# Queries, keys and gates of passes 1 to 3 as products of rounded halves, a later GpSimd modulation, and another order at the end of the attention passes

## What is computed

```python
mod = (silu(c) @ wmod).reshape(4, 6, 1, 256)            # sa, ca, ga, sb, cb, gb
h = layernorm(x) * (1 + ca) + sa
q, k, v = h @ wq + bq, h @ wk + bk, h @ wv + bv          # 16 heads of 16
scores = einsum('bhnd,bhmd->bhnm', q, k) * dmask         # gamma_h ** (n - m), n >= m
ret = einsum('bhnm,bhmv->bhnv', scores, v)
norm = (ret - mean) * rsqrt(var + eps) * gn_w + gn_b     # per head, over tokens and features
x = x + ga * ((silu(h @ wg + bg) * norm) @ wo + bo)
h = layernorm(x) * (1 + cb) + sb
top, index = top_k(h @ gate_kernel, 2)                   # softmax over the two
x = x + gb * sum_e combine_e * (silu(h @ w0_e) * (h @ w1_e)) @ wo_e
```

## Time and profile before

| what | us |
|---|---|
| median of three runs | 408.42 (404.41 to 411.78) |
| the profiled execution | 404.26 |
| its span, first to last instruction | 402.4 |
| TensorE busy | 361.0 |
| VectorE busy | 259.8 |
| GpSimd busy | 231.3 |
| ScalarE busy | 173.4 |

### The profile page before, as it was taken

The page is one execution under the profiler, slowest core; times in us unless marked ns, Lnnn a source line. Parts: engine busy times, 40 slices in busy tenths (PEclk is TensorE's granted clock), DMA queues, the critical chain, the costliest instruction groups (busy, mean ns, idle before and its releaser), DMA issues.

```text
span 402.4 us, 11502 instructions
## 1 busy us (share of the span) xinstructions
PE 361.0 (90%) x3893; PEld 269.8 (67%) x3894; DVE 259.8 (65%) x728; ACT 173.4 (43%) x264; POOL 231.3 (57%) x173
## 2 busy tenths in 40 slices
PE   3897899899899878898995999999999999999980
PEld 3474556766766656556562778888888888888860
DVE  6458528756955884947662577777777777777740
ACT  3424336444463313352122265555555555555510
POOL 3112610754781746186574377777777877777751
PEclk9999999999999998999997999999999999999995
DMA  6955090165447433254696343333344343333222
GB/s 218 307 182 187 11 332 5 54 211 210 154 165 243 164 102 104 66 212 118 140 347 140 66 75 75 62 71 76 79 79 79 79 79 79 71 69 72 40 27 25
DMA packets 32322, 49.05 MB, mean 122 GB/s; under 512 B 3198, under 2 KB 18972, under 8 KB 32284
## 3 DMA queue, kind: packets, MB, share of 16 engines
q1 hardware_dynamic: 11384, 16.98, 15.7%
q0 software_dynamic: 8176, 13.65, 15.2%
q10 hardware_dynamic: 12724, 17.89, 13.2%
HBM read 30.35 MB, written 18.16 MB: 121 GB/s over the span
## 4 chain that ended last, share of the span: by engine, by line
PE 44%; DMA 4%; DVE 2%; issue 2%; POOL 2%; ACT 1%; POOLq 1%; ACTq 0%; SPq 0%; DVEq 0%
PE ps L1719 15%; PE ps L1700 7%; PE ps L1699 7%; PE ps L1703 7%; PE ps L1711 4%; PE ps L1690 3%; DMA out_dram<-wg_s,qd 2%; PE ps L1606 2%; DMA routed<-z 1%; POOL routed L567 1%; DMA out_dram<-wg_s,wv_s 1%; DMA rowbuf<-routed 1%; ACT h_last L712 1%; DVE vd L1111 0%; POOLq L130 0%
## 5 line engine op out<-in xcount | busy, mean ns | idle before, releaser
L599 POOL TENSOR_TENSOR w_lo<-we,w_hi 128x1024 fp32r<-128x1024 f32 x31 | 77.0, 2484 | 25.2 <-ACT w_hi L825 23.0
L1719 PE MATMUL ps<-we,qeo 128*128 x312 | 76.5, 388 | 2.2 <-DVE wg_s L1317 1.3
L1719 PEld LDWEIGHTS ps<-we,qeo 128*128 128x128 f32 x312 | 57.3, 191 | 20.3 <-issue 13.4
L809 ACT COPY qeo<-ps 128x512 f32<-128x512 f32 x39 | 22.9, 587 | 111.0 <-PE ps L1711 111.0
L609 POOL DMA_INDIRECT out_dram<-wg_s,qd x30 | 46.9, 1563 | 34.3 <-issue 14.6
L1324 DVE TENSOR_TENSOR w_halves<-we,w_halves 128x1024 fp32r<-128x1024 f32 x31 | 38.0, 1225 | 8.3 <-ACT w_halves L825 8.3
L1296 DVE CAST rT_halves<-ps 128x256 fp32r<-128x256 f32 x31 | 13.2, 424 | 39.7 <-PE ps L1606 39.7
L567 POOL DMA_INDIRECT routed<-h_first,idx x24 | 24.9, 1038 | 15.3 <-DVE idx L1158 8.6
L825 ACT CAST w_hi<-we 128x1024 fp32r x31 | 32.6, 1052 | 0.0
L825 ACT CAST w_halves<-we 128x1024 fp32r x31 | 32.5, 1048 | 0.1
L1690 PE MATMUL ps<-we,xn 128*128 x64 | 31.9, 623 | 0.3 <-issue 0.3
(11 more groups left out here) (237 smaller groups left out, 709.0 us busy)
## 6 DMA issues: line engine op xcount, KB each, us to landing
rowbuf<-routed SPq DMA_DIRECT2D x37, 260.5 KB, 3.0
we<-in_ffn_w_kernel_dram ACTq DMA_DIRECT2D x16, 512.0 KB, 4.3
we<-in_ffn_wo_kernel_dram ACTq DMA_DIRECT2D x8, 512.0 KB, 6.7
routed<-z ACTq DMA_DIRECT2D x9, 260.5 KB, 4.0
xs<-in_attn_x_dram SPq DMA_DIRECT2D x4, 512.0 KB, 11.3
out_dram<-xs ACTq DMA_DIRECT2D x4, 512.0 KB, 3.6
we<-in_wmod_dram SPq DMA_DIRECT2D x1, 1024.0 KB, 10.4
sbcb<-gsc_dram SPq DMA_DIRECT2D x4, 256.0 KB, 4.8
```

What stands on the lines that cost most here:

```text
L599: g.tensor_tensor(w_lo[1], expert_up(e, 1), w_hi[1].bitcast(F32), ALU.subtract)\
L1719: last = mm(down_ps, eit[s % 2][:, k, :], weights(e, 2 * FT * F + k * D, D), start=k == 0, stop=k == KF - 1)
```

## The change

Queries, keys and gates of passes 1 to 3 (all but the last gate projection of pass 3) are computed from rounded halves. In pass 0 ScalarE copies the three weights to a rounded form (`projection_halves`) and GpSimd makes their remainders (`weight_remainders`). In each later pass ScalarE makes rounded features `hT_hi` ahead of `hT`, and VectorE the remainder `hT_lo` (`features_lo`), behind the second masks. `project_halves` is six matmuls. The halves lie in the places of experts 6 and 7, which are loaded only after the first gate of pass 3; TensorE's wait for the experts moves accordingly. GpSimd waits for `hT_lo` ahead of `modulate` in passes 1 and 2, and in pass 0 ahead of `scale_wo`.

The order also changes: `values(p, 0)` goes ahead of the first query; in pass 3 `second_normed` goes ahead of the first row loads, `table_rows(0)` behind the second masks, `values(3, 1)` ahead of `turn_h2`, and `turn_rows(0, 0)` behind `average`; `group_center` goes ahead of `take_rows(0, 0)`, `weighted(1, 1)` ahead of `choose_weights`, and the padding copies come four and four, after steps 4 and 5.

```diff
...
         w_hi, w_lo = [w0_halves[:, 0, :], w1_hi[:, :]], [w0_halves[:, 1, :], w1_lo[:, :]]
+        proj_hi = half("proj_hi", [P, 3, FT, D], "we", WE * (E - 1))
+        hT_hi = half("hT_hi", [P, FT, S], "we", WE * (E - 1) + 3 * FT * D)
+        hT_lo = [half("hT_lo0", [P, S], "we", WE * (E - 1) + 3 * FT * D + FT * S),
+                 half("hT_lo1", [P, S], "we", WE * (E - 1) - S)]
+        proj_lo = half("proj_lo", [P, 3, FT, D], "we", WE * (E - 1) - S - 3 * FT * D)
         eth, ein = ([smf[:, v, u * F:(u + 1) * F] for u in range(2)] for v in range(2))
...
         added, added_ok, pool_passed, act_passed = sems("added added_ok pool_passed act_passed")
+        proj_hi_ready, proj_lo_ready, ht_hi_ready, ht_ready, ht_lo_ready = sems(
+            "proj_hi_ready proj_lo_ready ht_hi_ready ht_ready ht_lo_ready")
         rt_hi, w_hi_ready, w_lo_ready = sem("rt_hi"), sems("w0_hi_ready w1_hi_ready"), sems("w0_lo_ready w1_lo_ready")
...
+            def weight_remainders():
+                for u, w in enumerate((wq_s, wk_s, wg_s)):
+                    pool.wait_ge(proj_hi_ready, u + 1)
+                    g.tensor_tensor(proj_lo[:, u, :, :], w[:, :, :], proj_hi[:, u, :, :].bitcast(F32),
+                                    ALU.subtract).then_inc(proj_lo_ready, 1)
             def decay_q(b, ft):
...
                     for later in range(1, B):
+                        if later == B - 1:
+                            weight_remainders()
                         first_scale(later)
                     pool.wait_ge(wo_in, 16 * 2)
+                    pool.wait_ge(ht_lo_ready, FT)
                 scale_wo(b)
...
                 if p >= 0:
+                    if b < B - 1:
+                        pool.wait_ge(ht_lo_ready, FT * (b + 1))
                     modulate(p)
...
+            def projection_halves():
+                act.wait_ge(setup_pe, 5)
+                for u, w in enumerate((wq_s, wk_s, wg_s)):
+                    a.copy(proj_hi[:, u, :, :], w[:, :, :]).then_inc(proj_hi_ready, 1)
             def features(b):
+                if b:
+                    for ft in range(FT):
+                        act.wait_ge(front.full, front.filled(b, f"hT{ft}"))
+                        a.activation(hT_hi[:, ft, :], front.bank(b, f"hT{ft}")[:, :], ACT.Identity,
+                                     scale=ca1T[:, ft, b:b + 1], bias=saT[:, ft, b:b + 1]).then_inc(ht_hi_ready, 1)
                 for ft in range(FT):
...
                     a.activation(hT[:, ft, :], front.bank(b, f"hT{ft}")[:, :], ACT.Identity,
-                                 scale=ca1T[:, ft, b:b + 1], bias=saT[:, ft, b:b + 1])\
-                        .then_inc(front.drained["act"], 1)
+                                 scale=ca1T[:, ft, b:b + 1], bias=saT[:, ft, b:b + 1]).then_inc(ht_ready, 1)
+                    act.wait_ge(ht_hi_ready, FT * b)
+                    act.wait_ge(ht_ready, FT * b + ft + 1)
+                    act.sem_inc(front.drained["act"], 1)
...
                 queries(b, 0)
-                if b == B - 1:
-                    act.wait_ge(gb_out, 16)
-                if b:
+                if 0 < b < B - 1:
                     load_expert(2 * b)
...
                 keys(b, 0)
-                if b:
+                if 0 < b < B - 1:
                     load_expert(2 * b + 1)
...
                 gate(b, 0)
+                if final:
+                    act.wait_ge(gb_out, 16)
+                    load_expert(2 * b)
+                    load_expert(2 * b + 1)
                 if not final:
...
                     gate(b, 1)
+                if b == 0:
+                    projection_halves()
+                if p >= 0:
+                    second_normed(p)
                 if final:
                     first_rows()
-                if p >= 0:
-                    second_normed(p)
                 if not final:
...
             act.dma_start(routed[PAD_ROW:PAD_ROW + P, :], tmpl).then_inc(tmpl_out, 16)
-            pads(range(0, 3))
+            pads(range(0, E // 2))
             act_step(5, 5)
-            pads(range(3, 6))
-            act_step(6, 6)
-            pads(range(6, E))
-            run_steps(act, act_step, first=7)
+            pads(range(E // 2, E))
+            run_steps(act, act_step, first=6)
...
                 v.tensor_tensor_scan(flat[0], flat[1], flat[2], 0.0, ALU.mult, ALU.add).then_inc(state_ready, 1)
+            def features_lo(b):
+                for ft in range(FT):
+                    dve.wait_ge(ht_ready, FT * b + ft + 1)
+                    v.tensor_tensor(hT_lo[ft][:, :], hT[:, ft, :], hT_hi[:, ft, :].bitcast(F32), ALU.subtract)\
+                        .then_inc(ht_lo_ready, 1)
...
                     attention_out(p)
-                if last:
-                    table_rows(0)
                 if not last:
...
                 masks(b, 1)
+                if not last:
+                    features_lo(b + 1)
+                if last:
+                    table_rows(0)
...
-            def dve_step(i, s, hidden_made=False, between=None):
+            def dve_step(i, s, hidden_made=False, weighted_made=False, between=None):
                 const = isinstance(i, int)
...
                     hidden(i - 1, s - 1)
-                if not (const and not 0 <= i - 2 < N_TILES):
+                if not weighted_made and not (const and not 0 <= i - 2 < N_TILES):
                     weighted(i - 2, s - 2)
...
             group_stats(b)
+            group_center(b)
             take_rows(0, 0)
-            group_center(b)
             gates(b, 1)
...
             choose_places(b)
+            weighted(1, 1)
             choose_weights(b)
-            dve_step(3, 3, hidden_made=True)
+            dve_step(3, 3, hidden_made=True, weighted_made=True)
             places(b)
...
                 last.then_inc(front.full, 1)
+            def project_halves(b, w, u, ft):
+                n = f"{w}{ft}"
+                wait(pe, front.free(b, n))
+                if b == 1:
+                    pe.wait_ge(proj_lo_ready, u + 1)
+                dst, cols = front.bank(b, n)[:, :], slice(ft * P, (ft + 1) * P)
+                for k in range(FT):
+                    mm(dst, proj_hi[:, u, k, cols], hT_hi[:, k, :], start=k == 0, stop=False)
+                    mm(dst, proj_lo[:, u, k, cols], hT_hi[:, k, :], start=False, stop=False)
+                pe.wait_ge(ht_lo_ready, FT * b)
+                for k in range(FT):
+                    last = mm(dst, proj_hi[:, u, k, cols], hT_lo[k][:, :], start=False, stop=k == FT - 1)
+                last.then_inc(front.full, 1)
+            def query(b, ft):
+                project_halves(b, "q", 0, ft) if b else project(b, "q", wq_s, ft)
+            def key(b, ft):
+                project_halves(b, "k", 1, ft) if b else project(b, "k", wk_s, ft)
+            def gate(b, ft):
+                project_halves(b, "g", 2, ft) if b else project(b, "g", wg_s, ft)
...
                 p, final = b - 1, b == B - 1
-                wait(pe, front.drains(b, "hT1"))
-                project(b, "q", wq_s, 0)
+                if p >= 0:
+                    values(p, 0)
+                    pe.wait_ge(ht_hi_ready, FT * b)
+                else:
+                    wait(pe, front.drains(b, "hT1"))
+                query(b, 0)
                 if p >= 1:
                     router(p - 1)
-                if p >= 0:
-                    values(p, 0)
                 if b == 0:
...
                     pe.wait_ge(vec_ready, 1)
-                project(b, "q", wq_s, 1)
-                project(b, "k", wk_s, 0)
+                query(b, 1)
+                key(b, 0)
                 if p >= 1:
...
                     values(p, 1)
-                project(b, "k", wk_s, 1)
+                key(b, 1)
                 if final:
...
                     mod_rows()
+                wait(pe, front.drains(b, "hT1"))
                 rows_v(b, "v01", 0)
...
                     pe.wait_ge(wg_in, 16)
-                project(b, "g", wg_s, 0)
+                gate(b, 0)
                 if b == 0:
...
                 else:
-                    project(b, "g", wg_s, 1)
+                    gate(b, 1)
                 if p >= 0:
...
                     values(b, 0)
+                    values(b, 1)
                 else:
...
                     turn_h2(p)
-            values(B - 1, 1)
-            turn_rows(0, 0)
...
             b = B - 1
-            pe.wait_ge(we_in, 16 * 3 * E)
             pe.sem_inc(it_full, 2)
...
             average(b)
+            turn_rows(0, 0)
             router(b - 1)
             average_dev(b)
+            pe.wait_ge(we_in, 16 * 3 * E)
             pe_step(0, 0, before_down=lambda: rank(b - 1))
...
```

## The result

The changed kernel takes **414.27 us** (median of four runs, 412.61 to 416.80) against 408.21 for the kernel before: ratio 1.0198, 95% interval 1.0144 to 1.0252. The forecast was 402, with a range to 409. The profiled execution takes 412.61 us, its span is 410.8, and its mean granted clock is 0.947. TensorE is busy 365.3 us, 4.3 more than before, although the projections became cheaper.

The account below looks back on a forecast made before the run. TensorE was taken to bound the attention stages. Terms -2.0 + 0.4 + 1.1 - 3.0 - 1.7 = -5.2 us against the profiled 404.26 gave 399.1, 403.2 against the median; predicted 402, nearer the median, range 394 to 409.

Parts of the forecast that it names:

- The loads of experts 6 and 7 start after this gate ... hidden, with little to spare: Pass 3: 3 MB of expert loads take 17 us, hidden behind the work before the first expert tile.
- A collision with the scatters: Rival: expert loads meet pass 3's scatters, layernorm's rows or tile 0 come 2 to 3 us later; 402 us, chance 0.08.
- End of pass 3, "3.0 saved": Before the first expert tile: layernorm before row loads, values(3,1) fills the gap, faster turn; 3.0 us saved, bounds 1.5 and 3.5.
- Pass 1, "2.0 us saved": Pass 1: no wait for hT and cheaper projections net 1.3 us, two gate projections 0.66; 2.0 us saved.
- Passes 2 and 3, the held modulation: GpSimd's held modulations delay VectorE's msk to 88.6, rank by 1.1 us; 0.4 lost in pass 2, 1.1 in pass 3.
- The sign that the prediction asked for in pass 2: TensorE idle 1 to 2 us before rank in passes 2 and 3; no wait there would mean the forecast fails.
- the forecast's 2.57 us for the chooser: Pass 2: VectorE's time from the router's logits to msk, 82.68 to 85.25 in the profile before.
- "The clock falls": Rival: TensorE's clock falls after the stall at rank, TensorE idling 1.9 us before rank, 1.2 before the average; chance 0.12.
- Pass 0, costed at nothing: Pass 0: three ScalarE copies and three GpSimd subtractions fall where those engines wait for input; cost nothing.
- The cover named in the prediction: Pass 0: ScalarE's and GpSimd's input waits hide the copies and subtractions; without it they cost about 2 us.
- Early tiles, "1.7 saved": Early expert tiles: weighting tile 1 earlier saves 0.9 us, earlier padding copies 0.8; 1.7 saved, bounds 0 and 4.
- Tile 8 is bound by a scatter: Early tiles: GpSimd's last scatter, priced at a padding copy's 4.00 us, lands at 213.4, against 214.2 for the last padding copy.

Follow-up runs that it names:

- e5_late_loads: Kernel before, with only the six loads of experts 6 and 7 moved behind the first gate of pass 3: 411.19 us, ratio 1.0137.
- e4_no_load67: Changed kernel without the late loads; ScalarE copies the weights of experts 4 and 5 to the places of 6 and 7: 409.59 us, ratio 1.0078.
- e7_two_passes: Changed kernel with halves in passes 1 and 2 alone, experts 6 and 7 loaded where they were before: 407.11 us, ratio 1.0007.
- e9_later_loads: Changed kernel with the loads of experts 6 and 7 moved behind the second layernorm of the last pass: 410.71 us, ratio 1.0121.
- e8_made_unused: Changed kernel with halves made and held for in passes 1 and 2 but every projection in float32, loads as before: 407.83 us, ratio 1.0033.
- e2_order: Kernel before with the new order alone; no halves, no hold, loads at the old places: 405.70 us, ratio 0.9950.
- e10_order_values: Kernel before with the new order alone, except values(p, 0) put back behind the router: 405.52 us, ratio 0.9985.
- e6_no_hold: Changed kernel without GpSimd's holds for the feature remainders in passes 0, 1 and 2: 418.97 and 424.08 us.
- e1_float32: Changed kernel with every projection in float32 again; halves still made, hold and late loads kept: 415.79 us, ratio 1.0219.

## Why the prediction was wrong

**The step that failed** is "The loads of experts 6 and 7 start after this gate ... hidden, with little to spare". It asked only whether 3 MB would arrive before the first expert tile, and they did: issued from 138.1, the last landed at 154.0, 15.9 us where 17 were forecast, and TensorE never waited for an expert's weights. What it left out is what TensorE itself does while the DMA engines are full (a share of 1.02 from 139 to 151.5). e5_late_loads shows the cost without the rest of the change (1.4%), e4_no_load67 takes the loads out (1.2 points back), e7_two_passes puts them back where they were (ratio 1.0007).

From the average to the first tile the changed kernel's profile needs 7.4 us more than that of e4_no_load67. Idle time ended by "issue" is 2.8 of it (5.3 against 2.5 from 138 us on). Another 3.5 is the clock of 0.50: `out_rows` 4.53 instead of 3.72, scores 2.66 instead of 1.62, the next 146 matmuls of `values` 2.68 instead of 2.15, the last gate 2.95 instead of 1.88. Of these, the 0.8 of `out_rows` can't be laid on the loads: e7_two_passes and e9_later_loads have a longer fall at that place (6.8 us from 139.3 and from 137.2) without them.

**A collision with the scatters** was a rival, at 2 to 3 us. The layernorm did wait for a scatter (150.01; about 1.0 us after its own input from GpSimd), but TensorE was later still, at 158.95. e9_later_loads took that collision away and the first tile came 1.3 us sooner, with the same stretch from the average (38.06 us against 37.97).

**End of pass 3, "3.0 saved"**: right about the wait, incomplete about the stretch. The idle 3.70 us ahead of `turn_h2` are gone in every version with the new order. From the average to the first tile e8_made_unused needs 29.36 us (130.10 to 159.46) and e4_no_load67 30.53, against 32.44 before: 3.1 and 1.9 saved, inside the bounds of 1.5 to 3.5. But e2_order (32.77), e10_order_values (33.98) and e7_two_passes (35.65) saved nothing, though they have no late loads either: their idle "issue" time is 3.2, 5.2 and 4.3 us instead of 0.9, and e7_two_passes loses 2.6 more in `out_rows`. The forecast has no term for such idle time at all; the late loads are only a part of what it left out.

**Pass 1, "2.0 us saved"**: 2.1 from `turn_x(1)` to `turn_x(2)`, the wait for `hT` gone. It was right in sum and not in every part: at full clock six matmuls took 1.36 us (q1, 50.67 to 52.03) where 1.44 was forecast, but q0 ran at a clock of 0.50 (48.34 to 50.67, 2.33 us).

**Passes 2 and 3, the held modulation**: right. From `turn_x(2)`, `msk` ends 11.7 us later; the forecast's 88.6 less 76.81 is 11.8. Rank came 12.08 after it, 1.4 later than before (10.72), where 1.1 was forecast. In pass 3 it idles 1.20 us for `msk`. The sign that the prediction asked for in pass 2, TensorE idle before rank, is missing, since the clock made TensorE equally late. `oh` was not held: it fell into the 0.38 us that GpSimd idled between the two `decay_q`. Beside GpSimd's instructions `vd` took 0.47 instead of 0.17, `msk` 1.13 instead of 0.19 and the two remainders of e6_no_hold 4.69 instead of 1.38; `ixf`, a cast with one input, waited too (0.66, where it takes 0.17 in e6_no_hold away from GpSimd's work). Before, `ixf` already took 0.63 beside a `decay_q`, so the forecast's 2.57 us for the chooser were not free of GpSimd.

**"The clock falls"** as a rival had a chance of 0.12 and a place behind the stall at rank, and the 406 among the range's cases was its time. No run shows such a fall: in pass 3 of the changed kernel TensorE idled 1.20 us before rank and 1.18 before the average, and the granted clock stayed at 1.00 (116 to 128 us). It fell elsewhere: for 3.4 us at 46.8, at 84.3 and at 111.7, none of them behind a stall at rank. It may be what eats much of the gain of cheaper products: e7_two_passes against e8_made_unused shows 1.1 of 4.0 us, inside the noise, and it has the same three falls (47.1, 84.7, 112.0). With float32 products there was no such fall in these passes (e1_float32) or one (e8_made_unused at 77.0, e10_order_values at 76.9). But e9_later_loads, with products in halves, has only one (82.5). Whether and how the stream of halves lowers the clock stays open.

**Pass 0, costed at nothing**: 1.0 lost, of which 0.4 is shown to be the change's. Scores start 0.6 late already (37.96 against 37.36), before the first of the weights' remainders (39.58). Then these stretch VectorE's gates, and the second masks come later still:

```profile
42.04 1.74 POOL L528 TENSOR_TENSOR proj_lo<-wg_s,proj_hi 128x512 fp32r<-128x512 f32 x1
```

```profile
41.55 1.09 DVE L1075 SCALAR_TENSOR_TENSOR z<-sm,z 128x512 f32<-128x512 f32 x1
```

```profile
45.38 0.83 PE L1461 MATMUL ps<-ident,xn 128*128 128x128 f32 x5 [1.50 <-DVE sm L1085]
```

The gates' product takes 1.09 instead of 0.68 beside a subtraction of 1.74, `turn_x(1)` idles 1.50 us for the masks instead of 0.44, and 1.02 us instead of 0.51 went to "issue". With the same pass 0, `turn_x(1)` starts at 44.53 in e9_later_loads and at 45.76 in e7_two_passes, so the rest may be chance. The cover named in the prediction was input waits of ScalarE and GpSimd; VectorE beside them was not looked at.

**Early tiles, "1.7 saved"**: 1.1 lost. Tile 8 is bound by a scatter, as forecast, but in the chain of waits (it answers to the earlier trace rows) neither term is left:

```profile
198.22 4.18 DMA out_dram<-wg_s,qd
...
216.67 5.41 DMA routed<-h_last,idx
...
223.59 2.62 DMA rowbuf<-routed
226.26 0.69 PE ps L1674 x2
```

Weighting tile 1 earlier did at its place what was forecast: TensorE waits 0.40 us for it instead of 1.31.

```profile
197.67 1.99 PE L1789 MATMUL ps<-we,qeo 128*128 x8 [0.40 <-DVE wg_s L1360]
```

But the last scatter is issued 49.84 us behind the first tile, where it was 49.33 before, since an accumulation of another tile's rows (4.18 us to land) now holds the chain. And it lands after 5.41 us; the forecast priced it by a padding copy's 4.00.

**The sum by halves of the change.** The order gives -0.5% (e2_order; nearly the same order in e10_order_values shows no gain beyond its interval); making and holding the halves takes 0.8 back (e8_made_unused), using them gives 0.3 (e7_two_passes), and the third pass with the late loads that it needs costs 1.9 (the changed kernel). Of that, the loads are 1.2 (e4_no_load67); the 0.7 left, third pass's halves and ScalarE's copy in e4_no_load67, was not taken apart. The 0.3 and the 0.7 lie inside the intervals. That e9_later_loads is 0.8 points better than the changed kernel, with the same stretch to the first tile and intervals that touch, stands in its profile in the passes, which are 0.9 to 1.4 us ahead from `turn_x(1)` on, though the code there is the same; the runs don't say why.

## What to carry to other kernels

A transfer is not hidden because it arrives in time: ask also what the engine that should hide it does meanwhile, above all one that works through blocks of many small instructions (here a stop of 1.55 us in a block of 112 matmuls, at a DMA share of 1.02), and leave room for its stops there even without the transfer (2.24 us in e7_two_passes). Memory that is borrowed from a later load moves that load, so price the new place of the load (1.2 points here) before the gain from the memory. And when a product gets cheaper, look at the granted clock of its stretch (0.92 instead of 1.00 in pass 2) before counting the gain.

## What the runs showed of the hardware

TensorE's idle time ended by "issue", summed from 138 us to the first expert tile, is 4.3 us in e5_late_loads, 5.3 in the changed kernel, 5.7 in e9_later_loads and 9.1 in e1_float32, all with late loads; without them 0.9 in the kernel before, 2.4 in e8_made_unused, 2.5 in e4_no_load67, 3.2 in e2_order, 4.3 in e7_two_passes and 5.2 in e10_order_values. So the loads are not its only source: the stop of 2.24 us in e7_two_passes stands at a DMA share of 0.27. What sets the loads apart is the packet that they delay by 3.9 to 4.6 us and the stop behind it. With loads issued from 137 to 144 us (the changed kernel, e1_float32, e5_late_loads) the granted clock then stood at 0.50 for 13.7 us in all three kernels, starting 2.0 to 3.7 us after TensorE's stop in `from_states` began; in the other kernels named here the falls from 137 us to the first tile lasted 3.4 or 6.8 us each, or there was none (e8_made_unused).

With products in halves the granted clock of the changed kernel's profile was 0.95 and 0.92 over passes 1 and 2, where the same kernel with float32 products kept 1.00 (e1_float32). A fall between 82 and 86 us stands in all five profiles used here that have products in halves (84.3 in the changed kernel, 83.6 in e4_no_load67, 85.7 in e6_no_hold, 84.7 in e7_two_passes, 82.5 in e9_later_loads) and in none of the six with float32 products; these are single executions, and e8_made_unused and e10_order_values have a fall at 77.
